# Attention's products with v as 64x64 tiles on TensorE, with v read where it was written

## The reference

```
qkv = layernorm(x) @ Wqkv.T + bqkv              # 16 heads of 16
q = (elu(q) + 1 + 1e-4) / sqrt(16);  k = elu(k) + 1 + 1e-4
kv_cumsum = cumsum(einsum('blhe,blhf->blhef', k, v), axis=1)
k_cumsum  = cumsum(k, axis=1)
num = einsum('blhe,blhef->blhf', q, kv_cumsum)
den = einsum('blhe,blhe->blh', q, k_cumsum)
out = layernorm((num / (den + 1e-4)) @ Wout.T + bout) * gamma + beta
x = x + out
```

## Time and profile before

| | |
|---|---|
| three executions | 2227.97, 2228.23, 2228.61 us (median 2228.23) |
| profiled execution: span from the first to the last instruction | 2226.0 us, that is 2.2 us below the median; what lies around the span is not in the profile |
| mean granted TensorE clock over the span | 0.994 of full speed |
| busy share of the span | PE 95%, DVE 93%, POOL 85%, ACT 83% |
| share of the hardware DMA queue (of 16 engines' span) | 48.2% |

### The profile page before, as it was taken

The page is one execution under the profiler, slowest core; times in us unless marked ns, Lnnn a source line. Parts: engine busy times, 40 slices in busy tenths (PEclk is TensorE's granted clock), DMA queues, the critical chain, the costliest instruction groups (busy, mean ns, idle before and its releaser), DMA issues.

```text
span 2226.0 us, 90845 instructions
## 1 busy us (share of the span) xinstructions
PE 2120.2 (95%) x30384; PEld 1488.7 (67%) x30384; DVE 2060.1 (93%) x5231; ACT 1849.7 (83%) x3880; POOL 1897.2 (85%) x3002
## 2 busy tenths in 40 slices
PE   3899999999999899999999999969999999999998
PEld 1566666666666678888888888855656665666665
DVE  7999999999999689999999999978999999999997
ACT  7888888888888688888888888868888888888884
POOL 6899999999999677888888888868989999999996
PEclk9999999999999999999999999999999999999999
DMA  4765555555556433333333333324655555555555
GB/s 104 128 121 115 116 112 112 116 116 114 113 112 110 81 65 71 72 72 72 72 70 72 72 72 70 72 54 80 114 112 112 113 113 113 112 113 113 113 116 112
DMA packets 740337, 217.67 MB, mean 98 GB/s; under 512 B 670497, under 2 KB 740001, under 8 KB 740257
## 3 DMA queue, kind: packets, MB, share of 16 engines
q1 hardware_dynamic: 740256, 216.68, 48.2%
HBM read 20.38 MB, written 16.78 MB: 17 GB/s over the span
## 4 chain that ended last, share of the span: by engine, by line
DVE 38%; PE 20%; issue 12%; SPq 11%; POOL 11%; DMA 4%; DVEq 2%; ACT 1%; POOLq 0%; ACTq 0%
DVE ffn_y L748 10%; DVE ffn_per_block L717 8%; DVE ffn_hx L710 7%; PE ffn_ps_gu L860 6%; SPq L1028 5%; SPq L1034 4%; POOL ffn_h_hl L790 4%; POOL ffn_h_hl L791 4%; PE attn_ps_qk L1254 3%; DVE ffn_q L744 3%; PE ffn_ps_down L872 3%; DMA attn_xT<-attn_x_hl 3%; SPq L1040 2%; PE attn_ps_num L1293 2%; DVE ffn_scale L723 2%
## 5 line engine op out<-in xcount | busy, mean ns | idle before, releaser
L860 PE MATMUL ffn_ps_gu<-wgu_hi,ffn_xT 128*128 128x512 f16 (+1 forms) x3072 | 737.6, 363 | 17.7 <-DVE ffn_hx L710 7.5
L860 PEld LDWEIGHTS ffn_ps_gu<-wgu_hi,ffn_xT 128*128 128x128 f16 x3072 | 300.8, 98 | 303.6 <-issue 22.0
L806 ACT ACTIVATE ffn_quarter<-ffn_y,offsets 128x960 int16<-128x960 f32 (+2 forms) x264 | 282.6, 1071 | 185.0 <-DVE ffn_y L748 184.9
L860 PE MATMUL ffn_ps_gu<-wgu_lo,ffn_xT 128*128 128x512 f16 (+1 forms) x1536 | 431.0, 362 | 0.0
L872 PE MATMUL ffn_ps_down<-wd_hi,ffn_hT 128*128 128x256 f16 x2816 | 351.1, 273 | 18.9 <-DVE x_sb L737 13.6
L790 POOL TENSOR_TENSOR ffn_h_hl<-ffn_q,ffn_h_scale_hi 128x704 f16<-128x704 f16 x256 | 352.2, 1376 | 12.5 <-DVE ffn_h_scale_lo L754 8.4
L791 POOL TENSOR_TENSOR ffn_h_hl<-ffn_q,ffn_h_scale_lo 128x704 f16<-128x704 f16 x256 | 354.0, 1383 | 0.0
L872 PEld LDWEIGHTS ffn_ps_down<-wd_hi,ffn_hT 128*128 128x128 f16 x2816 | 265.7, 98 | 99.6 <-issue 37.0
L717 DVE TENSOR_REDUCE ffn_per_block<-ffn_hx 128x60 f32<-128x960 f32 (+2 forms) x264 | 298.4, 1130 | 21.3
L748 DVE TENSOR_TENSOR ffn_y<-ffn_hx,ffn_per_block 128x960 f32<-128x960 f32 (+2 forms) x264 | 295.3, 1119 | 0.0
L842 ACT ACTIVATE ffn_odd<-ffn_quarter,offsets 128x960 f16<-128x960 int16 (+2 forms) x264 | 278.7, 1056 | 10.5 <-POOL ffn_shift L783 10.5
(11 more groups left out here) (183 smaller groups left out, 5081.5 us busy)
## 6 DMA issues: line engine op xcount, KB each, us to landing
attn_v_eo<-attn_v_nat SPq DMA_DIRECT2D x512, 34.0 KB, 1.9
x_sb<-in_L_attn_x SPq DMA_DIRECT2D x128, 128.0 KB, 2.5
out<-x_sb SPq DMA_DIRECT2D x128, 128.0 KB, 2.1
ffn_xT<-ffn_x_hl SPq DMA_TRANSPOSE x256, 2.4
ffn_hT<-ffn_h_hl SPq DMA_TRANSPOSE x256, 3.5
attn_xT<-attn_x_hl SPq DMA_TRANSPOSE x128, 2.4
attn_oT<-attn_o_hl SPq DMA_TRANSPOSE x128, 2.4
x_sb<-in_L_ffn_w_gate SPq DMA_DIRECT2D x2, 352.0 KB, 5.0
```

The lines of the kernel that those rows point to most:

```text
L806: nc.scalar.activation(quarter[:, back], y[:, back], ACT.Identity, bias=offsets[:, 0:1], scale=4.0 / HALF_MIN).then_inc(S["quarter"], 1)
L860: last = nc.tensor.matmul(ps_gu[par][:, a:b], xT[par][:, c, :], w[:, k, a:b], start=(n == 0), stop=(n == len(terms) - 1))
```

## The change

A product with v now takes one head instead of two: the 64 partitions that hold this head's keys, all 64 queries of the half, and 17 columns. That makes 32 products of 64x64 weights with 17 columns in place of 32 of 128x32 with 34. The keys of parity a lie on partition half a. Where half s of the tile equals a, v is already on these partitions in `v_nat` and is read there. For the other two of the four quarters, two DMAs (instead of four) copy v to the other partition half, into `v_cross`. `v_eo` goes away, with its zeros. Because `v_nat` is now read later, it has four buffers, and the step's phase counts modulo 4. Two waits ahead of the writing of `v_nat` are removed on ScalarE.

The order on TensorE becomes: the 16 products in which the partition half a equals the output's group g, then the products with the states (8, as before), then a wait of TensorE for its own last product of these (`same_rows`, a new semaphore), then the 16 products in which a differs from g, and then `num_done`. One more `sem_inc` stands ahead of the first 16. The diff, cut to its core (elsewhere `par` is derived from `phase`, and calls pass it on):

```diff
-ATTN_PLACES = {... "v_nat": (23296, 24384), "v_eo": (25472, 27648), ...
+ATTN_PLACES = {... "v_nat": (23296, 24384, 27648, 28736), "v_cross": (25472, 26016), ...
@@ attention
-        v_nat = pair("v_nat", [P, 2, HEADS // 2, VW])
-        v_eo = pair("v_eo", [P, 2, 2, HEADS // 2, VW])
+        v_nat = [at(f"attn_v_nat{j}", ATTN_PLACES["v_nat"][j], [P, 2, HEADS // 2, VW]) for j in range(PHASES)]
+        v_cross = pair("v_cross", [P, HEADS // 2, VW])
@@ sync_step
                 freed(sp, "num_done", tv, 2)
                 sp.sem_inc(S["turn"], 1)
-                for s in range(2):
-                    for a in range(2):
-                        sp.dma_start(v_eo[oth][half(a), s, a], v_nat[oth][half(s), a]).then_inc(S["v_eo" + even_odd], 16)
+                for a in range(2):
+                    sp.dma_start(v_cross[oth][half(a)], v_nat[(phase + 1) % PHASES][half(1 - a), a]).then_inc(S["v_cross" + even_odd], 16)
@@ gpsimd_step
-                for j in range(2):
+                for j in range(PHASES):
                     nc.gpsimd.memset(v_nat[j][:], 1.0).then_inc(set_up, 1)
-                    nc.gpsimd.memset(v_eo[j][:], 0.0).then_inc(set_up, 1)
@@ scalar_step
                 ready(act, "v_done", tf)
-                freed(act, "kv_done", tf, 2)
-                if not (isinstance(tf, int) and tf < 2):
-                    placed(act, tf - 2, oth)
-                nc.scalar.activation(v_nat[oth][:]...
+                nc.scalar.activation(v_nat[(phase + 1) % PHASES][:]...
@@ tensor_step
-                placed(pe, tn, oth)
+                crossed(pe, tn, oth)
...
             if valid(tn, N):
+                pe.sem_inc(S["turn"], 1)
+
+                def own_keys(c, j, a, g):
+                    for s in range(2):
+                        v = v_nat[(phase - 1) % PHASES][half(a), a] if s == a else v_cross[oth][half(a)]
+                        last = nc.tensor.matmul(num[half(s), g, c * PAIRS + j * 2 + a, :], scores[half(a), g, c, s, j, :], v[:, c * PAIRS + g * 2 + j, :],
+                                                start=(c == 0 and j == 0 and a == g), stop=(a != g), skip_group_check=True)
+                    return last
+
                 for c in range(DC):
-                    for r in range(PAIRS):
-                        for u in range(4):
-                            s, m = u // 2, u % 2
-                            h = c * PAIRS + r % 2 * 2
-                            nc.tensor.matmul(num[quarter(u), r // 2, h:h + 2, :], scores[:, r // 2, c, s, r % 2, quarter(m)], v_eo[oth][:, s, :, c * PAIRS + r, :],
-                                             start=(c == 0 and r % 2 == 0), stop=False, skip_group_check=True)
+                    for j in range(2):
+                        for a in range(2):
+                            own_keys(c, j, a, a)
                 for c in range(DC):
                     for s, st in enumerate((before, mid)):
                         for g in range(2):
                             last = nc.tensor.matmul(num[half(s), g, c * PAIRS:(c + 1) * PAIRS, :], q_feat[oth][half(g), c, half(s)], st[oth][half(g), c],
-                                                    start=False, stop=True, skip_group_check=True)
+                                                    start=False, stop=False, skip_group_check=True)
+                last.then_inc(S["same_rows"], 1)
+                ready(pe, "same_rows", tn)
+                pe.sem_inc(S["turn"], 1)
+                for c in range(DC):
+                    for j in range(2):
+                        for a in range(2):
+                            last = own_keys(c, j, a, 1 - a)
                 last.then_inc(S["num_done"], 1)
```

More of the change, by code:

```diff
@@ L79 @@
 ATTN_TURN = 4
+PHASES = 4
 def in_order(eng, step, first, end):
     for i in range(first, end):
-        step(eng, i, i % 2)
+        step(eng, i, i % PHASES)
 def in_turns(eng, step, first, end, turn):
@@ L90, in in_turns @@
         for k in range(turn):
-            step(eng, i + k, (first + k) % 2)
+            step(eng, i + k, (first + k) % PHASES)
 FIRST, DEPTH = 12, 6
@@ L107, in stages @@
     for k in range(2 * ahead + 1):
-        ffn_0(eng, N + DEPTH - 2 * ahead - 1 + k, (k + 1) % 2)
-        attn(eng, k - ahead, k % 2)
+        in_order(eng, ffn_0, N + DEPTH - 2 * ahead - 1 + k, N + DEPTH - 2 * ahead + k)
+        in_order(eng, attn, k - ahead, k - ahead + 1)
     attn_end = loop_end(ahead, ahead + 1, ATTN_TURN)
@@ L113, in stages @@
     for k in range(7):
-        attn(eng, N + ahead - 7 + k, (N + ahead - 7 + k) % 2)
-        ffn_1(eng, k - 6, k % 2)
+        in_order(eng, attn, N + ahead - 7 + k, N + ahead - 6 + k)
+        in_order(eng, ffn_1, k - 6, k - 5)
     in_order(eng, ffn_1, 1, first)
@@ L699, in sync_step, with vector_step @@
                 sp.dma_start(out_t[to], x_sb[:, to, :]).then_inc(stored, 16)
-        def vector_step(dve, i, par):
+        def vector_step(dve, i, phase):
+            par = phase % 2
             oth = 1 - par
@@ L878 @@
 ATTN_SEMS = ("sums", "stats", "var", "rstd", "shift", "xn", "x_hi", "x_split", "turn", "xT_even", "xT_odd", "qk_done", "relu", "exp", "feat", "k_even", "k_odd",
-             "q_feat", "q_rows", "v_done", "v_nat", "v_eo_even", "v_eo_odd", "kT_done", "k_nat", "scores_done", "masked", "kv_done", "kv_first", "kv_second",
-             "mid", "before", "num_done", "den", "rden", "o_ready", "o_hi", "o_split", "oT_even", "oT_odd", "proj_done",
+             "q_feat", "q_rows", "v_done", "v_nat", "v_cross_even", "v_cross_odd", "kT_done", "k_nat", "scores_done", "masked", "kv_done", "kv_first", "kv_second",
+             "mid", "before", "same_rows", "num_done", "den", "rden", "o_ready", "o_hi", "o_split", "oT_even", "oT_odd", "proj_done",
              "z_sums", "z_stats", "z_gamma", "x_beta", "consts", "w_turned")
@@ L920 @@
 ATTN_PLACES = {"o": 8352, "oT": (1024, 2048), "o_hl": (9376, 4096), "mid": (5632, 6176), "before": (6720, 7264), "first": 7808, "second": 11264, "k_nat": 12352, "zg": 13376,
-               "k_eo": (15104, 17152), "scores": 19200, "v_nat": (23296, 24384), "v_eo": (25472, 27648), "q_feat": (29824, 30848), "q_rows": (31872, 33920),
+               "k_eo": (15104, 17152), "scores": 19200, "v_nat": (23296, 24384, 27648, 28736), "v_cross": (25472, 26016), "q_feat": (29824, 30848), "q_rows": (31872, 33920),
                "expo": (35968, 38016), "xT": (40064, 41088), "x_hl": (42112, 43136), "xn": 44160,
@@ L1016, in turned_before, with sync_step @@
                 turned(eng, name, t - 2, par)
-        def sync_step(sp, i, par):
+        def sync_step(sp, i, phase):
+            par = phase % 2
             tx, tv, to, oth = i + 3, i + 1, i - 1, 1 - par
@@ L1210, in scalar_step @@
                 ready(act, "v_done", tf)
-                freed(act, "kv_done", tf, 2)
-                if not (isinstance(tf, int) and tf < 2):
-                    placed(act, tf - 2, oth)
-                nc.scalar.activation(v_nat[oth][:].rearrange("p a j w -> p (a j) w")[:, :, 0:E], blocks(ps_v), ACT.Copy, scale=unscale[:, 0:1]).then_inc(S["v_nat"], 1)
+                nc.scalar.activation(v_nat[(phase + 1) % PHASES][:].rearrange("p a j w -> p (a j) w")[:, :, 0:E], blocks(ps_v), ACT.Copy, scale=unscale[:, 0:1]).then_inc(S["v_nat"], 1)
                 ready(act, "relu", tf)
@@ L1319, in tensor_step @@
                             j = c * PAIRS + g * 2
-                            own_v = v_nat[par][half(s), :, j:j + 2, :].rearrange("p a j w -> p j a w")
+                            own_v = v_nat[phase][half(s), :, j:j + 2, :].rearrange("p a j w -> p j a w")
                             last = nc.tensor.matmul(half_state(s)[half(g), c * PAIRS * VW:(c + 1) * PAIRS * VW].rearrange("p (j a w) -> p j a w", a=2, w=VW),
```

34 lines of the change are left out of this document (20 added, 14 removed).

## The result

The changed kernel takes 2270.55 us (median of four executions, 2269.23 to 2271.74) against 2228.1 us before (four, 2227.89 to 2228.61): 1.0193 times as long, 95% interval 1.0181 to 1.0205. It is slower, by 42 us. The forecast was slower by 55, at 2284 us, with a range of 2242 to 2312. The profiled execution's span went from 2226.0 to 2267.8 us.

The account below looks back on a forecast made before the run. SP's queue was taken to bound the attention pass at 5.61 us a step; afterwards the DVE and TensorE loop at 6.04 (3.81 + 0.42 + 0.04 + 1.72 + 0.05). Over 128 steps +55 us gave 2284 us, range 2242 to 2312.

Parts of the forecast that it names:

- The wait of TensorE for itself: In the num section, between state products and second half: 0.10 us taken, plus 0.05 for loading weights again.
- Weights set the pace: Loading 64 weight columns paces the products with v: 0.057 us per group of four; chance 0.70, with wait 0.1 to 0.3.
- The floor of 60 cycles: Trainium skill's rule for short products: some 60 cycles of overhead per matmul, estimated at 0.025 us per group.
- The circle: DVE and TensorE loop: denominator to masking, num section, next denominator; 5.47 us a step before, 6.04 predicted after.
- The sum: A step of 6.04 us in place of 5.61: +0.43 for each of 128 steps, +55 us, forecast 2284 us.
- SP's queue sets the pace: Claim that SP's full queue bounds the old attention pass at 5.61 us a step, with TensorE waiting for turned x.
- Two other bounds lie close below: Prediction step naming TensorE alone, about 5.35 us, and the DVE and TensorE loop, 5.47, below SP's 5.61.
- the ring over POOL and the turned x: Absent from prediction: loop from num through DVE, POOL's `o_split`, SP's transposes, turned x to TensorE; 22.42 us per four steps.
- the rival in which columns set the pace: Products with v: 17-column groups take 0.017 us, weights hidden; section 1.16, time 2212 us, faster; chance 0.06.
- floor: Rival: a fixed cost per short product, 0.025 us a group; section 1.27, time 2226 us; chance 0.03, shared with mixtures.
- half way: Rival: groups of products with v keep 0.038 us; section 1.45, +22 us, time 2250 us; chance 0.13.
- The dear wait: Rival: TensorE's wait for itself costs 0.42 us, groups 0.06; step 6.40, +102 us, time 2330 us; chance 0.07.

## Why the prediction was right, and where it wasn't

**The wait of TensorE for itself: right, and the largest term.** The prediction's sum has 0.22 for the last state product, 0.10 for the wait and 0.05 for weights, 0.37 from start to start; its list of what would show it says 0.3, which doesn't follow from that sum. Measured: 0.395. The timeline splits it: the last state product starts at 1103.43 and lasts 0.22, from its end to the weights at 1103.80 pass 0.15, and 0.03 more to the product. So the wait with its weights took 0.18 where 0.15 was predicted; the rest is the product's own length, which elsewhere overlaps the next. The Trainium skill, page "TensorEngine Tiling (Array Packing)", "Gotcha 1: PSUM Pressure", says why it is there: tiles on different rows of the array may not write one PSUM bank at the same time, and software has to see to it. No run here let them.

**Weights set the pace: right.** 58 ns for a group of four records against 57 taken; 34 columns left it, 32 weight columns brought it to 32. The floor of 60 cycles that the Trainium skill states on the page "TensorEngine Tiling (Array Packing)", section Performance Considerations, doesn't set it. By my estimate from that figure it would be 25 ns for a group whatever the weights are; the groups measured 58 and 32 ns and followed the weight columns.

**The circle: right, by a hair.** 6.04 was predicted, 5.99 measured; TensorE alone 5.92 predicted, 5.94 measured. That second agreement is in part luck: with 5.40 for the kernel before, as found above, in place of 5.35, the same sum gives 5.97. The terms of the circle: 3.81 and 3.80 measured; from masking to the first product 0.46 with the added `sem_inc`, measured 0.36; section and denominator 1.77, measured 1.82. The 0.42 of the prediction came from one step. In the changed kernel the masking is the last to come in every step, but in two of every four steps three more instructions of TensorE's sequencer follow the wait for it, and 0.42 us pass to the product, while in the other two only one follows, and it is 0.25 and 0.35. DVE's wait ahead of the denominator was expected at about 0.7 and came to 0.89.

**The sum: 55 us predicted, 42 measured.** (2281 and 2.2 make 2283; the 2284 is a slip of one.) 128 x 0.05 = 6 of the missing 13 us is the step's size. The rest, 128 x 0.38 = 49 against 42, is the few steps at the pass's ends, which I took as equal to the others: "In the few steps at the pass's ends, shared with feed-forward steps, I take the same". They added less: the first 13 steps from the pass's first masking on took 0.8 us less in all than before, where 13 x 0.38 = 5 us more were reckoned.

**"SP's queue sets the pace": incomplete.** The queue was full, as the earlier trace rows say, but leaving two copies out left the step at 5.60. The step that fell short is "Two other bounds lie close below", which names TensorE alone and the DVE-TensorE circle: the ring over POOL and the turned x is missing, and it lay between, at the same 5.6. So 5.61 - 5.47 holds as the most that can be gained, but taking load off SP alone gained nothing of it in mid-pass. This cost the forecast nothing, since the section grew past both; the 2212 given to the rival in which columns set the pace counts on the same gain. SP was expected to wait for `num_done`; it waits for `o_split`, one semaphore further.

**The rivals.** Columns, floor and half way fell with the groups at 58 ns. The dear wait fell too: a step of 6.40 would have needed 0.42 for the semaphore alone, and 0.15 passed from the last product's end to the next weights.

Not tried: the changed products in a kernel with both of the old bounds relieved, so what the change costs there, where a step takes 5.47, stays open; other work of TensorE put into the hole; the pace of 64 weight columns with another order of tiles.

## What to carry to other kernels

A queue that never waits is full, but that doesn't make it the only bound: follow the chain of waits once around before pricing its relief, and take the relief of both bounds together. When short products are cut into more weight columns and fewer moving ones, compare the weight loads with each other first: they may already set the pace. A wait of TensorE for its own last product cost the whole overlap of two products here, not only a semaphore, so an order of products that needs one has to earn it elsewhere on TensorE.

## What the runs showed of the hardware

- A group of four records of fp32 products (two products, each of which leaves two records) on 64x64 tiles comes 58 ns after the last, with 17 and with 34 moving columns; on 64x32 tiles 32 ns. A weight load's record is 134 and 108 ns long.
- A product's wait for TensorE's own last product opened 0.395 us from start to start, where 0.02 is usual.
- A change of the tile shape between fp32 products cost about 0.1 us (110 ns against 9 to 16, and 128 against 16), each time.
- A copy of 34 KB and one of 17 KB cost SP's queue the same 0.6 us to issue.
- The same 64x136 fp32 copy took 493 ns on POOL and 307 on ScalarE.
